# A four-layer attention and mixture-of-experts kernel: layers 2 to 4 of a pair as one instruction stream per batch instead of one for both

## The chip, the cores and the metric

The kernel runs on one core of a Trainium2 chip. A core has four compute engines that run their own instruction streams side by side: PE (TensorE, matrix products and transposes into PSUM banks), DVE (VectorE), ACT (ScalarE, activation functions and copies) and POOL (GpSimd). SP (SyncE) computes nothing here; its stream issues the DMA transfers. The streams meet only through semaphores: an instruction increments one when it is done, another engine waits for a value.

The metric is the device time of one execution, in microseconds (us), as the median of several runs.

## What is computed

Eight batches, each of 128 rows of width 128, go through four layers in fp32. A layer is a cross-attention on a context of 120 rows (x) and a feed-forward part (f). Cut to what matters:

```python
def layernorm(x): return (x - mean(x)) / sqrt(var(x) + 1e-5)

# for each of the 8 batches; ctx is [120, 128]
x = x + attention1(q=ctx @ .., k=ctx @ .., layernorm(x))              # L0X: one head
n = layernorm(x)                                                       # L0F: 8 heads x 8 experts
gate_v, gate_o = top2_sigmoid(n @ sel_v), top2_sigmoid(n @ sel_o)      #   [128, 8 heads, 8 experts]
for h in range(8):
    v   = sum(gate_v[:, h, e] * (n @ v_w[h, e]) for e in range(8))     #   128x128 products
    o   = softmax(q_h @ k_h.T) @ v
    x  += sum((gate_o[:, h, e] * o) @ o_w[h, e] for e in range(8))
x = x + softmax_masked(16 heads of 8)(layernorm(x), ctx)               # L1X
x = x + LN(gelu(layernorm(x) @ ternary(W_fc))) @ ternary(W_proj)       # L1F
x = x + softmax_masked(2 heads of 64, q and k normalized)(..)          # L2X
n = layernorm(x)                                                       # L2F: 8 experts
x = x + sum(top2_softmax(n @ Wg)[:, e] * (gelu(n @ W1[e] + b1) @ W2[e] + b2) for e in range(8))
x = x + softmax(16 heads of 64, plus a bias)(layernorm(x), ctx)        # L3X
n = layernorm(x)                                                       # L3F: grouped top 2 of 8
x = x + routed_experts(n, sigmoid gates, best group of 2) + relu(n @ up)**2 @ down
```

## The kernel before

**Two halves and four pairs.** The eight batches are taken in four pairs; the two batches of a pair are called lanes 0 and 1. Layer 0 (L0X and L0F) is the front half of a pair, and the three other layers (L1X to L3F) are its back half. The two halves have buffers of their own: names with `f_` and `gated`, `weights`, `gates_of` belong to the front half, `bank`, `wide_a`, `wide_b`, `small`, `route` to the back half. So the front half of pair k+1 runs while the back half of pair k runs.

**What the front half is.** It opens with a chain of short dependent steps: layer norm (`f_xn`), attention of one head, layer norm, routing of 64 experts on DVE (`f_group`, `f_route`), softmax exponentials of 8 heads per lane on ACT (line 1039), then the gates are turned by PE (`f_gateT`), written to memory and read back broadcast over partitions (`gated<-gates_of`, 512 KB each). After this chain come the experts, 32 groups of gated products: DVE multiplies `gated` by `f_xnT`, PE runs 8 products of 128x128 for each. They are the bulk of PE's work.

**What the back half is.** `back_pair(pair)` of an engine writes the steps of both lanes in lockstep: each stage stands as `for lane in LANES`. Its softmaxes of 16 heads are 16 exponentials per lane on ACT (line 1103, one per head, with the row sum read out), the transposes and products of PE taken 4 heads at a time. L1F uses GELU (line 1155), L2F uses GELU with a bias in 16 pieces per lane (line 1211); GELU and exponential need different tables in ACT, and the compiler puts an ACT_TABLE_LOAD where they change. The routings of L2F and L3F are computed for both lanes by one set of small DVE instructions on tiles of 128x16 (`route`, `per_group`).

**What sets the order.** Each engine executes one stream. `front_steps()` is a generator that writes the front half of all pairs, with a `yield` after every step. `weave` returns `ahead()`, which stands between the steps of `back_pair`, and takes from the string `AHEAD` for this engine how many front steps are written at this place. So there are two sequences, front and back, and in the back one both lanes move together. The last pair's back half has no front half beside it: this stretch is called the tail.

**Before the first pair** stands a setup: folded weights of layer 0, and as late setup, woven with the front half of pair 0, the ternary weights of L1F (`abs_sum`, `threshold`, `w_L1f`), the mask lengths (`lens`, line 1604), `qkn`, and the products that belong to them (line 459, a helper through which most products go).

**Products that keep PE running.** `keep_warm` (its products go to `f_bank` out of `w_const`, 512 columns, with no reader) stands at five places of the tail, 11 products in all; two more products stand in the front half of pair 0, into `bank`.

**Transfers.** The context of the next pair is loaded for both lanes by one transfer (`ctx_back`, 120 KB), the result of a pair is stored by one (128 KB).

Of the kernel before, what the change touches and what calls it, by code (L numbers as in the profile page):

```python
# [6 lines left out]
ALU = mybir.AluOpType  # L7
# [34 lines left out]
AHEAD = {  # L42
# [28 lines left out]
def build(nc, x_in, ctx_in, q_mask, k_mask, pair_mask, packs, experts, gates_of, out):  # L71
    with ExitStack() as stack:
# [246 lines left out]
        with nc.Block() as block:  # L319
# [41 lines left out]
            def _(pe):  # L361
# [7 lines left out]
                for half in range(2):  # L369
# [5 lines left out]
                    last.then_inc(setup_products, 1)  # L375


        def weave(engine, steps):
            counts = iter(AHEAD.get(engine, "").split())

            def ahead():
# [1623 lines left out]
```

## Time and profile before

| | us |
|---|---|
| median of 3 runs | 759.89 (757.17 to 760.71) |
| the profiled execution | 758.24 |
| its span in the trace | 756.9 |
| busy in the span: PE | 680.3 (90%), 5496 instructions |
| busy: DVE | 495.9 (66%), 1289 instructions |
| busy: ACT | 369.6 (49%), 1281 instructions |
| busy: POOL | 188.8 (25%), 256 instructions |

The span is cut into nine stretches for reading: the start, with the front half of pair 0 alone up to 116 us; then three times a stretch in which the opening chain of the next pair's front half runs beside the first layers of the current pair's back half (116 to 168, 289 to 336, 458 to 507 us), each followed by one in which the front half's experts run beside the rest of the back half (168 to 289, 336 to 458, 507 to 626 us); and the tail (626 to 757 us). "PEclk" is the clock that the chip granted to PE, as a share of 2.4 GHz. A matrix product of fp32 stands in the trace as two PE instructions, a transpose as one.

### The profile page before, as it was taken

Reading aid. Unit: us, or ns where it says so; the run is one execution under the profiler, and the core shown is the slowest. Engines: PE = TensorE matmul, PEld = TensorE weight load, DVE = VectorE, ACT = ScalarE, POOL = GpSimd, SP = SyncE. Lnnn points to the kernel's source line nnn. Section 1 sums busy time; section 2 is a strip of 40 time slices with the busy share of each in tenths; the row PEclk is TensorE's granted clock in tenths of the full one; section 3 lists DMA queues with packets and bytes.
Section 4 is the critical chain, followed back from the end, with each engine's and each line's share of the span. In section 5 each row is a group of like instructions: output and inputs, shape, how many; then the busy total and the mean of one; then the engine's idle time right before and its main releaser. Section 6 shows DMA issues by size and latency. Waiting matters only on the chain.

```text
span 756.9 us, 14486 instructions
## 1 busy us (share of the span) xinstructions
PE 680.3 (90%) x5496; PEld 599.8 (79%) x5496; DVE 495.9 (66%) x1289; ACT 369.6 (49%) x1281; POOL 188.8 (25%) x256
## 2 busy tenths in 40 slices
PE   5759998899999898889999997999999996879887
PEld 4559996769999795759999995769999894557675
DVE  1946557948776848948767667858767477155635
ACT  2420204971363833971366535872365635636473
POOL 1000006342101606342201416423101407420130
PEclk9869998699999999899999998899999998899969
DMA  9659992039836511057833703049816400000000
GB/s 349 288 187 349 374 382 63 2 125 353 303 104 229 168 57 29 1 169 270 308 116 133 266 1 118 3 146 347 292 65 207 156 29 7 1 1 1 2 1 8
DMA packets 33189, 113.71 MB, mean 150 GB/s; under 512 B 3680, under 2 KB 7264, under 8 KB 32736
## 3 DMA queue, kind: packets, MB, share of 16 engines
q1 hardware_dynamic: 33120, 112.78, 42.3%
q8 instruction: 44, 0.72, 0.4%
q14 instruction: 25, 0.20, 0.1%
HBM read 111.72 MB, written 1.05 MB: 149 GB/s over the span
## 4 chain that ended last, share of the span: by engine, by line
PE 59%; DVE 18%; ACT 10%; POOL 5%; DMA 3%; issue 2%; SPq 0%; POOLq 0%; DVEq 0%
PE f_bank L459 29%; PE bank L459 26%; ACT wide_b L1103 4%; DMA gated<-gates_of 3%; DVE gated L1431 3%; PE bank L655 2%; DVE f_route L1431 1%; POOL rstd L1322 1%; DVE max_neg L1690 1%; DVE wide_b L1434 1%; DVE x L1434 1%; ACT f_b L1039 1%; ACT wide_a L988 1%; POOL wide_b L1331 1%; PE f_bank L552 1%
## 5 line engine op out<-in xcount | busy, mean ns | idle before, releaser
L459 PE MATMUL f_bank<-weights,gated 128*128 128x128 f32 x2048 | 245.2, 278 | 9.1 <-DVE gated L1431 8.8
L459 PEld LDWEIGHTS f_bank<-weights,gated 128*128 128x128 f32 x2048 | 237.0, 194 | 13.4 <-issue 11.4
L1103 ACT ACTIVATE wide_b<-wide_b,max_neg 128x120 f32<-128x120 f32 x272 | 103.6, 386 | 25.5 <-DVE max_neg L1690 19.7
L1322 POOL TENSOR_TENSOR rstd<-var_eps,w_const 128x1 f32<-128x1 f32 (+1 forms) x56 | 44.6, 796 | 253.4 <-DVE var_eps L1427 253.2
L1431 DVE TENSOR_TENSOR gated<-gated,f_b 128x1024 f32<-128x1024 f32 x64 | 81.5, 1296 | 29.0 <-ACT f_b L988 15.4
L1331 POOL TENSOR_TENSOR wide_b<-wide_b,row_inv 128x480 f32<-128x480 f32 x64 | 72.0, 1130 | 104.9 <-DVE row_inv L1695 104.7
L1431 DVE TENSOR_TENSOR gated<-gated,f_xnT 128x1024 f32<-128x1024 f32 x64 | 76.8, 1224 | 19.6 <-DMA gated<-gates_of 19.4
L988 ACT ACTIVATE wide_a<-bank 120x512 f32<-120x512 f32 (+4 forms) x109 | 57.3, 550 | 52.4 <-PE bank L655 14.4
L655 PE MATMUL bank<-w_const,wide_b 128*120 128x128 f32 x256 | 46.5, 323 | 13.2 <-POOL wide_b L1331 12.9
L1286 POOL TENSOR_TENSOR f_rstd<-f_var_eps,w_const 128x1 f32<-128x1 f32 x24 | 13.3, 559 | 175.3 <-DVE f_var_eps L1427 175.1
L1103 ACT ACTIVATION_READ_ACCUMULATOR wide_b<-wide_b,max_neg 128x1 f32 x272 | 52.2, 192 | 0.0
L655 PEld LDWEIGHTS bank<-w_const,wide_b 128*120 128x120 f32 x256 | 34.3, 162 | 22.5 <-issue 21.7
L1690 DVE TENSOR_REDUCE max_neg<-wide_b 128x4 f32<-128x480 f32 x64 | 41.8, 653 | 2.2
L988 ACT ACTIVATE xnT<-bank 128x128 f32<-128x128 f32 x48 | 12.1, 277 | 57.9 <-PE bank L644 57.7
L459 PE MATMUL bank<-wide_a,v 120*32 120x128 f32 (+1 forms) x512 | 37.2, 297 | 3.5 <-ACT wide_a L988 3.4
L988 ACT ACTIVATE f_v<-f_bank 128x512 f32<-128x512 f32 x16 | 9.5, 597 | 56.4 <-PE f_bank L459 56.4
L459 PEld LDWEIGHTS bank<-wide_a,v 120*32 120x32 f32 (+1 forms) x512 | 30.0, 134 | 8.9 <-issue 6.9
L1211 ACT ACTIVATE wide_a<-bank,w_L2f 128x128 f32<-128x128 f32 x128 | 34.3, 452 | 0.0
L459 PE MATMUL bank<-xnT,w_L2f 128*128 128x128 f32 x256 | 30.4, 276 | 0.0
L1431 DVE TENSOR_TENSOR x<-bank,x 128x128 f32<-128x128 f32 x24 | 6.9, 288 | 35.7 <-PE bank L459 35.6
L1434 DVE SCALAR_TENSOR_TENSOR wide_b<-bank,w_L3x 128x480 f32<-128x480 f32 x32 | 20.5, 639 | 14.8 <-PE bank L459 14.8
L1434 DVE SCALAR_TENSOR_TENSOR x<-bank,gate,x 128x128 f32<-128x128 f32 x64 | 22.4, 351 | 11.4 <-PE bank L459 9.6
(236 smaller groups left out, 1202.2 us busy)
## 6 DMA issues: line engine op xcount, KB each, us to landing
gated<-gates_of SPq DMA_DIRECT2D x128, 512.0 KB, 6.3
weights<-in_experts SPq DMA_DIRECT2D x64, 512.0 KB, 6.8
w_L2f<-in_L2f SPq DMA_DIRECT2D x1, 2124.0 KB, 15.0
w_L3x<-in_L3x SPq DMA_DIRECT2D x1, 2108.0 KB, 19.1
wide_b<-in_raw0f SPq DMA_DIRECT2D x1, 1024.0 KB, 5.6
w_L3f<-in_L3f SPq DMA_DIRECT2D x1, 1000.0 KB, 21.8
w_L1f<-in_L1f SPq DMA_DIRECT2D x1, 516.0 KB, 9.3
x_next<-in_x SPq DMA_DIRECT2D x4, 128.0 KB, 5.9
```

The lines of the kernel that those rows point to most:

```text
L459: return nc.tensor.matmul(o, lhsT, rhs, start=first, stop=last)
L552: last = nc.tensor.transpose(f_bank[lane][:, 128 * c:128 * c + 128], f_b[lane][:, 128 * h:128 * h + 128], ident)
L655: last = nc.tensor.transpose(bank[lane][(1, 2, 0, 1)[i]][0:K, 128 * c:128 * c + 128], wide_b[lane][:, K * h:K * h + K], ident)
L988: return nc.scalar.activation(o, i, ACT.Identity, bias=bias, scale=scale)
L1103: last = nc.scalar.activation(p, p, ACT.Exp, bias=max_neg[lane][:, h:h + 1], accum_out=row_sum[lane][:, h:h + 1])
L1211: last = nc.scalar.activation(wide_a[lane][:, at:at + 128], bank[lane][(1, 0, 2, 1)[i]][:, 128 * c:128 * c + 128], ACT.Gelu, bias=part["L2 ...
L1286: nc.gpsimd.tensor_tensor(f_rstd[lane][:, :], f_var_eps[lane][:, :], part["const", "minus_half"][:, 0:1], ALU.pow)\
L1322: nc.gpsimd.tensor_tensor(rstd[lane][:, cols], var_eps[lane][:, cols], part["const", "minus_half"][:, 0:cols.stop - cols.start], ALU.pow)\
L1331: nc.gpsimd.tensor_tensor(p3, p3, row_inv[lane][:, 4 * i:4 * i + 4].unsqueeze(2).broadcast_to([128, 4, K]), ALU.mult).then_inc(probs_norme ...
L1431: return nc.vector.tensor_tensor(o, a, c, op)
L1434: return nc.vector.scalar_tensor_tensor(o, a, scalar, c, op0, op1)
L1690: nc.vector.tensor_reduce(max_neg[lane][:, 4 * i:4 * i + 4], s3, AX.X, ALU.max, negate=True)\
```

## The change

1. Each engine's stream is woven out of three generators instead of two: the front half, and the back half of lane 0 and of lane 1. `ORDER` holds a string for each engine with one letter per step: `f`, `0` or `1`. The back half of a lane ends with pair k and goes on with pair k+1 without regard to the other lane.
2. `back_pair(pair)` becomes `back_lane(pair, lane)`. The order inside a lane's sequence is nearly the old one; on ACT the transposed probabilities are taken 2 pieces behind the exponentials of the same lane (before: 4 behind over both lanes), on DVE the inverse sums 1 behind (before: 2).
3. The routings of L2F and L3F are written for each lane on tiles of 128x8. Per pair L2F's goes from 19 to 30 DVE instructions and L3F's from 31 to 56, over four pairs 144 more. The step semaphores `max_taken` and `gate_ready` are kept for each lane.
4. `ctx_back` is loaded, and the output stored, for each lane (60 KB and 64 KB), with a semaphore of its own for each lane's load.
5. The 11 `keep_warm` products of the tail are gone. The two in the front half of pair 0 stay.
6. ACT_TABLE_LOADs in the stream of ACT: 17 before, 35 after. For the back halves of the four pairs 4, 4, 4 and 4 before; 10, 10, 8 and 6 after.
7. `pair_lens`, a small copy on POOL, is made for each lane (4 instructions more).

The diff, cut to its core:

```diff
-AHEAD = {
-    "PE": "10 6 5 15 28 0 8 0 0 5 0 2 0 1 2 2 1 0 2 0 1 2 0 0 0 0 0 7 0 0 1 0 2 1 2 1 3 1 0 0 0 1 1 0 0 0 1 0 0 "
...
+ORDER = {
+    "PE": "ffffff00fff0f0ffffffffffffffffffffffffffffffffffffffffffffffffffffff001010ff00ff1ff0ff100f00ff1ff01f"
...
-        ctx_back_loaded = sem("ctx_back_loaded")
+        ctx_back_loaded = [sem(f"ctx_back_loaded{lane}") for lane in LANES]
...
-        def weave(engine, steps):
-            counts = iter(AHEAD.get(engine, "").split())
-
-            def ahead():
-                for _ in range(int(next(counts, 0))):
-                    next(steps, None)
-
-            def rest():
+        def weave(engine, front, lane0, lane1):
+            streams = {"f": front, "0": lane0, "1": lane1}
+            for stream in ORDER.get(engine, ""):
+                next(streams[stream])
+            for steps in streams.values():
                 for _ in steps:
                     pass
-            return ahead, rest
...
+                    if pair + 1 < PAIRS:
-                        for lane in LANES:
-                            sp.wait_ge(kv_psum[lane], kv_psum.upto(L2X, 3, pair))
-                        cols = slice(2 * K * (pair + 1), 2 * K * (pair + 2))
-                        sp.dma_start(ctx_back[:, :], ctx_in[:, cols]).then_inc(ctx_back_loaded, 16)
-                        ahead()
+                        sp.wait_ge(kv_psum[lane], kv_psum.upto(L2X, 3, pair))
+                        cols = slice(K * (2 * pair + 2 + lane), K * (2 * pair + 3 + lane))
+                        sp.dma_start(columns(ctx_back, lane, K), ctx_in[:, cols]).then_inc(ctx_back_loaded[lane], 16)
+                        yield
...
-                    link(tt(as_lanes[3], as_lanes[3], of_lanes(part["const", "first"]), ALU.mult))
+                    link(tt(r[3], r[3], first, ALU.mult))
+                    yield
                     link(nc.vector.tensor_reduce(worth[1], halves[3], AX.X, ALU.max))
...
+                weave("DVE", front_steps(), back_steps(0), back_steps(1))
```

What the strings move is shown at three places. A name's last digit is the lane or, for `bank`, lane and bank; line numbers of the two kernels differ.

**DVE at the start**, where the late setup meets the front half of pair 0. Before, from the second lane's variance to the routing of layer 0:

```order
L1427 TENSOR_SCALAR f_var_eps_1<-f_mean_var_1 128x1
L1428 TENSOR_SCALAR f_xn_0<-f_x_0,f_mean_var_0,f_rstd_0 128x128
L1428 TENSOR_SCALAR f_xn_1<-f_x_1,f_mean_var_1,f_rstd_1 128x128
L1428 TENSOR_SCALAR threshold<-bank00 128x2
L1427 TENSOR_SCALAR threshold<-threshold 128x2 x2
L1427 TENSOR_SCALAR wide_a_1<-w_L1f,threshold 128x512
L1427 TENSOR_SCALAR w_L1f<-w_L1f,threshold 128x512
L1431 TENSOR_TENSOR w_L1f<-w_L1f,wide_a_1 128x512
```

Now, from the first row of the late setup to the first lane's `f_x`, which stands ahead of all the rows above except the setup's own:

```order
L1332 TENSOR_SCALAR threshold<-bank00 128x2
L1331 TENSOR_SCALAR threshold<-threshold 128x2 x2
L1331 TENSOR_SCALAR wide_a_1<-w_L1f,threshold 128x512
L1331 TENSOR_SCALAR w_L1f<-w_L1f,threshold 128x512
L1335 TENSOR_TENSOR w_L1f<-w_L1f,wide_a_1 128x512
L1331 TENSOR_SCALAR wide_a_1<-w_L1f,threshold 128x512
L1331 TENSOR_SCALAR w_L1f<-w_L1f,threshold 128x512
L1335 TENSOR_TENSOR w_L1f<-w_L1f,wide_a_1 128x512
L1372 RECIPROCAL f_row_inv_1<-f_row_sum_1 128x1
L1507 TENSOR_REDUCE lens<-wide_b_1 128x8 x2
L1338 SCALAR_TENSOR_TENSOR qkn<-w_L2x 128x1
L1338 SCALAR_TENSOR_TENSOR f_x_0<-f_bank0,f_row_inv_0,f_x_bias_0 128x128
```

The ternary weights have moved from behind the front half's second layer norm to ahead of it, and `lens` and `qkn`, which before stood behind the first `gated` tile, stand there too.

**ACT beside the opening chain of pair 1's front half** (`f_b` are its exponentials, `f_gateT` the gates' turn; the rest belongs to the back half of pair 0). Before:

```order
L1031 ACTIVATE f_group<-f_group 128x64
L1039 ACTIVATE f_b_0,f_row_sum_0<-f_bank0,f_max_neg_0 128x128 x4
L1039 ACTIVATE f_b_1,f_row_sum_1<-f_bank1,f_max_neg_1 128x128 x4
L1103 ACTIVATE wide_b_1,row_sum_1<-wide_b_1,max_neg_1 128x120 x4
L988 ACTIVATE wide_a_1<-bank12 120x512
L988 ACTIVATE wide_a_0<-bank00 120x512
L1039 ACTIVATE f_b_0,f_row_sum_0<-f_bank0,f_max_neg_0 128x128 x4
L1039 ACTIVATE f_b_1,f_row_sum_1<-f_bank1,f_max_neg_1 128x128 x4
L988 ACTIVATE f_gateT0<-f_bank0 128x128
```

Now:

```order
L975 ACTIVATE f_group<-f_group 128x64
L983 ACTIVATE f_b_0,f_row_sum_0<-f_bank0,f_max_neg_0 128x128 x4
L983 ACTIVATE f_b_1,f_row_sum_1<-f_bank1,f_max_neg_1 128x128 x4
L1089 ACT_TABLE_LOAD
L1089 ACTIVATE wide_b_0<-bank01 128x512
L932 ACTIVATE wide_a_0<-bank02 120x384
L932 ACTIVATE wide_a_1<-bank10 120x512
L983 ACT_TABLE_LOAD
L983 ACTIVATE f_b_0,f_row_sum_0<-f_bank0,f_max_neg_0 128x128 x4
L932 ACTIVATE wide_a_1<-bank11 120x512
L983 ACTIVATE f_b_1,f_row_sum_1<-f_bank1,f_max_neg_1 128x128 x4
L932 ACTIVATE f_gateT0<-f_bank0 128x128
```

Lane 0 is already in L1F when the second half of the front half's exponentials comes, so GELU stands between two groups of exponentials, with a table load on either side.

**PE in the tail, at L2F of the last pair** (`xnT` by `w_L2f` are the experts' first products). Before:

```order
L459 MATMUL bank01<-xnT_0,w_L2f 128x128 x4
L459 MATMUL bank11<-xnT_1,w_L2f 128x128 x4
L459 MATMUL bank00<-xnT_0,w_L2f 128x128 x4
L459 MATMUL bank10<-xnT_1,w_L2f 128x128 x4
L459 MATMUL bank02<-xnT_0,w_L2f 128x128 x4
L459 MATMUL bank12<-xnT_1,w_L2f 128x128 x4
```

Now:

```order
L460 MATMUL bank01<-xnT_0,w_L2f 128x128 x4
L460 MATMUL bank00<-xnT_0,w_L2f 128x128 x4
L777 MATMUL bank12<-w_const,wide_b_1 120x128 x2
L460 MATMUL bank02<-xnT_0,w_L2f 128x128 x4
L460 MATMUL bank11<-wide_a_1 128x128 x2
L460 MATMUL bank01<-xnT_0,w_L2f 128x128 x4
L460 MATMUL bank00<-w_L2f,wide_a_0 128x128 x8
L644 MATMUL bank10<-w_const,xn_1 128x128
```

Lane 0's experts stand beside the end of lane 1's L2X (turned probabilities, output product, layer norm), where before both lanes' experts stood side by side.

## Rows read from the trace of the kernel before

**Rows 1.** Busy time by stretch: start:end and length, each engine, PE clock, DMA.

```profile
core 0: us, PE busy (x) PEld busy (x) DVE busy (x) ACT busy (x) POOL busy (x), PEclk, DMA share, GB/s
0.00:60.00 60.00, 37.75 (x209) 32.60 (x210) 32.33 (x77) 18.32 (x66) 3.26 (x10) 0.83 0.72 270
60.00:116.00 56.00, 55.67 (x495) 55.35 (x494) 32.40 (x31) 5.08 (x10) 0.00 (x0) 1.00 0.99 374
116.00:168.00 52.00, 45.47 (x279) 34.18 (x278) 35.95 (x97) 38.50 (x151) 25.86 (x42) 0.84 0.14 39
168.00:289.00 121.00, 117.59 (x1081) 112.41 (x1082) 88.61 (x222) 52.49 (x168) 22.50 (x23) 1.00 0.57 197
289.00:336.00 47.00, 38.60 (x259) 28.59 (x260) 33.86 (x94) 35.40 (x146) 24.54 (x40) 0.93 0.16 41
336.00:458.00 122.00, 119.80 (x1097) 114.02 (x1095) 86.39 (x224) 55.34 (x172) 25.94 (x23) 1.00 0.53 185
458.00:507.00 49.00, 43.27 (x274) 31.24 (x275) 35.06 (x99) 38.27 (x151) 25.28 (x41) 0.86 0.24 70
507.00:626.00 119.00, 117.13 (x1085) 112.36 (x1083) 85.37 (x221) 52.28 (x167) 23.26 (x23) 1.00 0.53 188
626.00:757.00 131.00, 105.05 (x727) 79.10 (x726) 65.96 (x233) 73.93 (x253) 38.13 (x57) 0.86 0.01 3
```

**Rows 2.** DVE at the start in order of time: start, duration, instruction, idle before.

```profile
15.11 0.34 DVE L1428 TENSOR_SCALAR f_xn<-x_next,f_mean_var,f_rstd 128x128 f32<-128x128 f32 x1
...
21.07 0.35 DVE L1434 SCALAR_TENSOR_TENSOR f_x<-f_bank,f_row_inv,f_x_bias 128x128 f32<-128x128 f32 x1
...
24.12 0.15 DVE L1428 TENSOR_SCALAR threshold<-bank 128x2 f32<-128x2 f32 x1
...
28.14 0.41 DVE L1490 TENSOR_REDUCE f_group<-f_route 128x32 f32<-128x256 f32 x1
...
49.79 1.23 DVE L1431 TENSOR_TENSOR gated<-gated,f_xnT 128x1024 f32<-128x1024 f32 x1 [8.14 <-DMA gated<-gates_of]
50.94 2.21 DVE L1604 TENSOR_REDUCE lens<-wide_b 128x8 f32<-128x960 int32 x2
```

**Rows 3.** DVE, first and last instruction of pair 1's opening front chain.

```profile
120.21 0.34 DVE L1428 TENSOR_SCALAR f_xn<-x_next,f_mean_var,f_rstd 128x128 f32<-128x128 f32 x1
...
167.10 1.22 DVE L1431 TENSOR_TENSOR gated<-gated,f_xnT 128x1024 f32<-128x1024 f32 x1
```

**Rows 4.** The tail's chain of waits: shares by line, then pieces (start, length).

```profile
by line: PE bank L459 41.5%; ACT wide_b L1103 15.2%; issue 3.6%; PE bank L655 3.4%; POOL rstd L1322 2.4%; PE f_bank L459 2.0%; ACT wide_a L988 1.9%; DVE wide_b L1431 1.8%; DVE small L1917 1.6%; POOL wide_a L1339 1.5%; DVE stats L1626 1.2%; 
...
634.42 7.67 ACT wide_b L1103 x40
...
660.83 1.28 ACT L1155
662.13 0.61 ACT wide_b L1155
...
689.55 14.80 PE bank L459 x130
...
715.44 7.68 ACT wide_b L1103 x40
```

**Rows 5.** Busy time in short stretches, columns as in rows 1.

```profile
52.00:56.00 4.00, 4.00 (x21) 4.00 (x21) 4.00 (x6) 0.00 (x0) 0.00 (x0) 0.50 0.99 392
...
640.00:660.00 20.00, 16.87 (x107) 10.95 (x106) 6.60 (x21) 13.67 (x50) 10.59 (x18) 0.73 0.00 1
...
689.00:705.00 16.00, 15.51 (x136) 15.11 (x136) 7.91 (x33) 10.86 (x38) 0.00 (x0) 1.00 0.00 1
```

**Rows 6.** Groups of instructions: two of the tail, one of the whole span.

```profile
L459 PE MATMUL f_bank<-w_const 128*128 128x512 f32 x22 | 11.9, 663 | 0.0
...
L988 ACT ACTIVATE wide_a<-bank 120x512 f32<-120x512 f32 x16 | 9.0, 588 | 4.3 <-PE bank L655 4.2
...
L1431 DVE TENSOR_TENSOR route<-route,per_group 128x16 f32<-128x16 f32 x44 | 7.7, 175 | 1.5
```

More of the change, by code:

```diff
@@ new lines, in back_lane @@
+                    yield
+                    turn_x(lane, L3X, xn[lane])
+                    yield
+                    for half in range(2):
+                        pe.wait_ge(xnT_ready[lane], xnT_ready.upto(L3X, 1, pair))
+                        for c in range(4):
+                            at = 512 * half + 128 * c
+                            last = mm(bank[lane][1 + half][:, 128 * c:128 * c + 128],
+                                      part["L3x", "wq"][:, at:at + 128], xnT[lane][:, :])
+                        last.then_inc(q_psum[lane], 1)
+                        yield
@@ new lines, in back_lane @@
+                    last.then_inc(hidden_psum[lane], 1)
+                    yield
+                    pe.wait_ge(hidden_ready[lane], hidden_ready.upto(L3F, 3, pair))
+                    for c in range(4):
+                        mm(bank[lane][1][:, 0:D], wide_a[lane][:, 128 * c:128 * c + 128],
+                           part["L3f", "down"][:, 128 * c:128 * c + 128], c == 0, False)
+                    yield
+                    pe.wait_ge(hidden_ready[lane], hidden_ready.upto(L3F, 5, pair))
@@ L1169, in back_pair @@
-                    ahead()
+                        for n in range(4 + behind):
+                            if n < 4:
+                                exponentials(lane, layer, n, range(4 * n, 4 * n + 4))
+                                yield
+                            if n >= behind:
+                                take_transposed(layer, n - behind, lane)
+                                yield
+                    act.wait_ge(kv_psum[lane], kv_psum.upto(L1X, 1, pair))
+                    copy(small[lane][:, 128:128 + K], bank[lane][1][:, 0:K], bias=part["L1x", "bk"])\
+                        .then_inc(kv_ready[lane], 1)
@@ L1172, in take_keys_l3 @@
+                    act.wait_ge(turned_psum[lane], turned_psum.upto(L2X, 1, pair))
+                    copy(wide_a[lane][:, 1408:1408 + K], bank[lane][2][:, 0:K], scale=qkn[:, :])\
+                        .then_inc(turned_ready[lane], 1)
+                    yield
                     def take_keys_l3(half, lane):
@@ L1188, in back_pair @@
-                    ahead()
-                    for lane in LANES:
-                        exponentials(lane, L2X, 0, range(H2X))
-                    ahead()
-                    for lane in LANES:
-                        act.wait_ge(pT_psum[lane], pT_psum.upto(L2X, 1, pair))
-                        copy(wide_a[lane][0:K, 256:512], bank[lane][2][0:K, 0:256]).then_inc(pT_ready[lane], 1)
-                    ahead()
-                    for lane in LANES:
-                        take_xT(lane, L2F)
@@ new lines, in back_lane, with back_steps @@
+                    yield
+                    inverse_root(lane, L2X, 2, one)
+                    yield
+                    inverse_root(lane, L2X, 3, slice(0, 2))
+                    yield
+                    inverse_root(lane, L2F, 1, one)
+                    yield
+                    inverse_root(lane, L3X, 1, one)
+                    yield
+                    yield from normalise_probs(L3X)
+                    inverse_root(lane, L3F, 1, one)
+                    yield
+                def back_steps(lane):
+                    for pair in range(PAIRS):
+                        yield from back_lane(pair, lane)
@@ new lines, in back_lane @@
+                    for h in range(H2X):
+                        p = wide_b[lane][:, K * h:K * h + K]
+                        last = ts(p, p, row_ok[lane][:, 2 + h:3 + h], row_inv[lane][:, h:h + 1], ALU.mult, ALU.mult)
+                    last.then_inc(normed[lane], 1)
+                    yield
+                    add_output(lane, L2X, bank[lane][1][:, 0:D])
+                    yield
+                    norm_apply(lane, L2F)
+                    yield
+                    dve.wait_ge(gate_psum[lane], gate_psum.upto(L2F, 1, pair))
@@ L1872, in back_pair @@
-                    r = [route[:, i, 0:both] for i in range(7)]
-                    halves = [r[i].rearrange("p (g e) -> p g e", e=4) for i in range(7)]
-                    worth = [per_group[:, i, 0:4] for i in range(4)]
+                        yield from mix_half(half, lane)
+                        yield
+                    dve.wait_ge(out_psum[lane], out_psum.upto(L2F, 3, pair))
+                    x_done(lane, L2F, tt(x[lane][:, :], bank[lane][1][:, 0:D], x[lane][:, :], ALU.add))
+                    yield
```

1245 lines of the change are left out of this document (541 added, 704 removed), and 20 rows, old and new, of the table AHEAD.

## The prediction, made before the changed kernel ran

> **What bounds the kernel now.** I read the busy time by stretch first [rows 1], since the totals of a kernel with four repeated pairs mix places with different limits. There are three kinds. In the expert stretches (168 to 289, 336 to 458, 507 to 626, and 60 to 116) PE is busy 97 to 99% of the time at a clock of 1.00; DVE follows with at most 73%, ACT with 45%. PE is the bound there, and a change moves them only by the PE work that stands in them. In the three chain stretches (116 to 168, 289 to 336, 458 to 507) no engine is full: in the first PE has 45.47 of 52 us, at a clock of 0.84, ACT 38.50, DVE 35.95. What ends last is the opening chain of the next pair's front half, since no expert product can run before the first gated tile: in pair 1 from 120.21 to 167.10, 46.9 us [rows 3]. In pair 0, where nothing of a back half is beside it, the same chain runs from 15.11 to 49.79 [rows 2]: 34.7 us. So up to 12 us of each chain stretch is what the back half's steps put between the chain's, in the orders of ACT, DVE and PE. The third kind is the tail, 131 us with the last pair's back half alone: PE 105.05 busy, with 11.9 of it products that nobody reads [rows 6], ACT 73.93, DVE 65.96, clock 0.86. The chain of waits there [rows 4] goes to and fro: PE products 41.5%, exponentials 15.2%. Its long pieces are 40 ACT rows in 7.67 us (20 exponentials and their sums), 130 products in 14.80, 40 ACT rows in 7.68. Each of them carries both lanes' work, after which the other engines get going again: the lockstep is what makes the tail long.
>
> **The start, +5 us (0 to +7).** DVE makes the ternary weights in 4.0 us, from 24.12 to 28.14 [rows 2], in a place where the front half's routing was on its way through PE and ACT anyway; the f_group that follows is then ready without a wait. Now this work, `lens` (2.21) and `qkn` (0.15) stand ahead of `f_x_0`, which ran at 21.07. They begin when `abs_sum` has gone through PE. In the new order `abs_sum` can start after the first lane's maximum, and its product is not behind 512-column products any more, so the block can start near 20.9: 20.9 + 4.0 + 2.4 gives `f_x_0` near 27.3, 6.2 late. Behind it the chain is as before, but only 0.7 of setup work stands between it and f_group instead of 4.0, less about 2 us that the routing needs on PE and ACT after `f_xn`: late by 6.2 - 3.3 + 2 = 5 at f_group. The 2.4 us of `lens` that leave their old place behind the first gated tile [rows 2] return nothing, since PE there runs at a clock of 0.50 and is full [rows 5]. The lower end is that f_group waited for something else than DVE; the upper end is the full 6.2 and a little.
>
> **Expert stretches, -6.3 us.** I counted the PE work of both orders between a pair's first and last expert product, at 0.111 us an instruction (119.80 over 1097 gives 0.109, 14.80 over 130 gives 0.114, [rows 1, 4]). Before: 108.9, 111.2 and 108.9, together 329.0, for 358 us of trace, a factor of 1.09. After: 97.0, 108.1 and 118.1, together 323.2. The difference, 5.8, times 1.09 is 6.3. It is no work saved: back-half products have moved from these stretches into the chain stretches.
>
> **Chain stretches, -2 us (-12 to +10).** They get that work: 31.5, 30.0 and 32.2 before, 35.0, 33.0 and 31.9 after, where they have room (45.47 busy of 52, part of it at half clock). What decides is what stands on ACT between the chain's steps. Of the back half's exponentials, 0.384 us each with their sums (7.67 over 20, [rows 4]), there were 32 in each of the three; now 32, 16 and 16. Other copies of the back half, 0.59 at most [rows 6], were 7, 11 and 10, and are 20, 19 and 15. Pair 1: 13 copies at about 0.35 and two table loads of 1.28 [rows 4] are 7.1, of which some 2 are hidden by DVE and POOL steps of the chain: +5. Pair 2: -6.1 and +3: -3. Pair 3: -6.1 and +2: -4. The lower end is that all three come down to 43 us each, the upper that copies and table loads cost in full.
>
> **Table loads and routing in the expert stretches, +3 us (0 to +20).** Of the 18 new loads 2 are in the chain stretches, 2 in the tail; 14 are here, 18 us of ACT. The 144 new DVE instructions at 0.175 [rows 6] are 25 us, 19 of them here. ACT has 52.49 of 121 and DVE 88.61 of 121 busy [rows 1], so both fit under PE: the cover is that PE always has expert products or the other lane's to run. They cost only where PE's order has the next back-half product too early; +3 for that. Without this cover it would be 18 us.
> The Trainium skill ("ScalarE: Activation LUTs", "What ACT_TABLE_LOAD costs") puts a switch at 2.66 us, load and drain. By it 18 loads would be 48 us instead of 23. The trace doesn't agree for this kernel: the load at 660.83 took 1.28 and the GELU behind it began at 662.13 [rows 4]. The same page's "Table sets: the hidden batching unit" wants calls batched by set, and speaks against this change.
>
> **The tail, -15 us (-24 to -7).** `keep_warm` is 2.0% of the chain [rows 4], 2.6 us; two more table loads are 2.6: they cancel. What is left is the stagger: lane 0 is about half a layer ahead, so that lane 1's exponentials run while PE has lane 0's products. On the chain, the three long pieces lose their second half, (7.67 + 14.80 + 7.68) / 2 = 15.1. Shorter pieces lose theirs too, but the engines collide: ACT's 73.93 + 2.6 can't be undercut, and each lane's own chain is longer than that. I take the 15.1, a tail of 116. The lower bound is a tail of 107, the upper that half of the 15 is lost. The transfers per lane and the copies on POOL cost nothing: DMA is at 0.01 in the tail, 0.14 to 0.24 in the chain stretches [rows 1], where the context is needed. The last store is of 64 KB instead of 128.
>
> **The sum.** +5 - 6.3 - 2 + 3 - 15 = -15.3 on the profiled 758.24, so 742.9, a ratio of 0.980; on the median of 759.89 that is 744.5. I say **744**.
>
> **The rivals.**
> A, the forecast: 732 to 753. 0.42.
> B, the chain stretches come down to what the front half needs: with fewer exponentials before its gates, all three are 43 us instead of 46.9 and the like (-12 instead of -2), and the tail gives 20 and more. 744 - 10 - 6 = 728, 712 to 732. For it: pair 0's chain took 34.7. Against it: more PE and copy work now stands in these stretches. 0.24.
> C, the clock eats the tail's gain. After the 8.1 us in which DVE waited for the gates of pair 0, and PE for DVE [rows 2], PE ran at 0.50, at least from 52 to 56 [rows 5]; in the tail it was at 0.73 between 640 and 660 but at 1.00 in L2F's 16 us [rows 5], behind keep_warm products. Without these L2F and L3X could begin at 1.2 GHz: 14.8 us of products would take some 5 more, and as much again over the other places. 744 + 10 = 754, and up to 764 if in the middle the loads show too. 0.16.
> The Trainium skill ("TensorE: Matmul & The Clock Gate", "HAM oscillation") describes such falls of the clock in kernels whose PE idles between tiles. By it the removal of `keep_warm` costs; the removed products themselves are the 11.9 us of PE.
> D, slower: the fixed orders bind. One stream's step that isn't ready holds the two others on its engine. The price is the cover above: with two table loads and the routing of each lane held ahead of front steps in each pair, ACT and DVE steps that gate expert products come late, 18 us of loads that are no longer hidden, and the start's 5, with half the tail's gain left: 744 + 18 + 7.5 = 770. It decides as soon as PE's busy share in the expert stretches falls under 92%. Against it: 97% now, and DVE gets there only to about 78%. 0.18.
>
> **How the numbers follow.** Range for 8 in 10: from 718, inside B, to 764, the end of C; that leaves out D and the end of B. A alone is 732 to 753. A change of 0.5%, 3.8 us, is about what a measurement can tell from none. Faster by more than that (under 756.1): A, B and half of C, 0.71 with a little of D's near side. Same: the rest of C, and where D is mild, 0.12. Slower 0.17.
>
> **What would show it.** In the trace after: f_group of pair 0 near 33 instead of 28.14; first gated tile of pair 0 near 55. The expert stretches PE-busy over 96% at 1.00, about 2 us shorter each on average, the first shortest. Pair 1's opening chain longer than 46.9, those of pairs 2 and 3 shorter. Tail from the last expert product to the end 110 to 120 us, with L2F of lane 0 beside L2X of lane 1. Wrong would be: a tail over 125 (C, if its clock is under 0.8; else the chain of one lane is longer than I think), or PE idle in the expert stretches (D).

## The result, and the profile after

The changed kernel is slower by 1%: 767.0 us (764.7 to 771.6, 4 runs) against 759.8 for the kernel before (4 runs), a ratio of 1.010 with a 95% interval of 1.007 to 1.013. The forecast was 744, in a range of 718 to 764; the time lies outside, and on the other side of 759.8. The profiled execution took 764.72, with a span of 763.4.

The trace of the changed kernel, busy time by stretch, columns as in [rows 1]. The cuts are at its own first and last expert products, so the stretches are the same nine: start, experts of pair 0, then chain and experts three times, then the tail.

```profile
0.00:56.50 56.50, 31.69 (x163) 25.91 (x163) 26.65 (x72) 18.75 (x68) 3.26 (x10) 0.88 0.63 235
56.50:121.80 65.30, 63.54 (x546) 62.85 (x547) 38.63 (x35) 4.78 (x8) 0.55 (x1) 0.98 0.97 365
121.80:177.70 55.90, 45.70 (x307) 34.44 (x305) 39.46 (x117) 43.48 (x158) 27.03 (x46) 0.91 0.13 36
177.70:286.70 109.00, 104.70 (x943) 100.26 (x942) 79.92 (x199) 48.09 (x145) 17.13 (x17) 1.00 0.61 220
286.70:336.50 49.80, 41.55 (x319) 32.12 (x317) 38.25 (x123) 38.09 (x142) 20.63 (x35) 0.96 0.19 55
336.50:461.00 124.50, 117.89 (x1039) 110.58 (x1040) 89.39 (x231) 60.90 (x183) 27.83 (x29) 0.99 0.55 187
461.00:505.40 44.40, 38.51 (x311) 30.56 (x310) 36.49 (x123) 34.98 (x130) 19.13 (x31) 1.00 0.18 49
505.40:640.40 135.00, 130.40 (x1158) 119.94 (x1156) 99.50 (x268) 69.09 (x214) 32.43 (x37) 1.00 0.48 163
640.40:763.40 123.00, 95.44 (x702) 73.52 (x702) 73.11 (x268) 75.66 (x253) 37.43 (x57) 0.86 0.01 3
```

The kernel before has the same cuts at 51.2, 116.8, 168.5, 288.4, 336.6, 457.3, 507.7 and 625.9, close to those of [rows 1]. That gives the difference by stretch, and beside it what the prediction had:

| | before | after | difference | forecast |
|---|---|---|---|---|
| start and experts of pair 0 | 116.8 | 121.8 | +5.0 | +5 |
| chain stretches | 51.7, 48.2, 50.4 | 55.9, 49.8, 44.4 | -0.2 | -2 |
| expert stretches | 119.9, 120.7, 118.2 | 109.0, 124.5, 135.0 | +9.7 | -3.3 |
| tail | 131.0 | 123.0 | -8.0 | -15 |
| span | 756.9 | 763.4 | +6.5 | -15.3 |

Two rows of four are far off, and in both a gain is missing. In the expert stretches PE has fewer instructions (3140 against 3263 in [rows 1]) at the same clock, but hardly less busy time (353.0 us against 354.5), and it stands idle for 15.5 of 368.5 us, where in [rows 1] it is 7.5 of 362: PE's busy share fell from 97 or 98% to 95 to 97%. In the tail PE is only 95.44 busy, ten less than before, at the same clock of 0.86; the `keep_warm` products that are gone were 11.9 of it [rows 6]. (They stood at six places of the tail, two at each of five and one at the sixth, not at five places as the part on the kernel before has it.)

The start, in DVE's order of time (start, duration, instruction): what [rows 2] has at 21.07, 28.14 and 49.79.

```profile
27.24 0.34 DVE L1338 SCALAR_TENSOR_TENSOR f_x<-f_bank,f_row_inv,f_x_bias 128x128 f32<-128x128 f32 x1
...
32.84 0.42 DVE L1394 TENSOR_REDUCE f_group<-f_route 128x32 f32<-128x256 f32 x1 [0.33 <-ACT f_route L932]
...
55.11 1.23 DVE L1335 TENSOR_TENSOR gated<-gated,f_xnT 128x1024 f32<-128x1024 f32 x1 [8.76 <-DMA gated<-gates_of]
```

The three groups of table loads of largest cost in the view of groups, 29 of the 34 behind the first, and then the chain of waits of the second expert stretch where they stand thickest (start, length, what; a row "ACT L1135" without a name is a table load).

```profile
L1046 ACT ACT_TABLE_LOAD x12 | 15.4, 1283 | 0.2
...
L1135 ACT ACT_TABLE_LOAD x10 | 12.8, 1283 | 0.2
...
L1089 ACT ACT_TABLE_LOAD x7 | 9.0, 1283 | 0.1
```

```profile
415.90 3.13 ACT wide_b L1046 x16
419.03 0.19 ACT route L1128
419.22 0.02 issue
419.24 1.28 ACT L1135
420.52 0.01 issue
420.54 1.14 ACT wide_a L1135 x4
421.67 0.02 issue
421.69 1.28 ACT L1046
...
422.99 1.62 ACT wide_b L1046 x8
...
427.10 1.28 ACT L1135
...
428.39 3.20 ACT wide_a L1135 x12
```

One lane is in the softmax of L3X, the other in the GELUs of L2F, and ACT begins three table loads within 8 us, with the chain of waits on it without a break from 415.90 to 431.6. Over the whole span the chain holds 21 loads, 27 us; that of before holds 4, 5.1 us (the expectation of the second run below says 3).

### The profile page after: what moved, and what is told of

It is laid out like the page before. It is cut to its first block, busy times and chain, and to the rows that moved or that the text cites. A ratio compares the mean times of both kernels' runs of the same rounds, so it can differ in the third digit from the quotient of the medians.

```text
span 763.4 us, 14661 instructions
## 1 busy us (share of the span) xinstructions
PE 669.4 (88%) x5474; PEld 590.2 (77%) x5474; DVE 521.4 (68%) x1433; ACT 393.8 (52%) x1299; POOL 185.4 (24%) x260
## 4 chain that ended last, share of the span: by engine, by line
PE 54%; ACT 17%; DVE 15%; POOL 4%; DMA 4%; issue 3%; SPq 0%; DVEq 0%; POOLq 0%
PE f_bank L460 27%; PE bank L460 22%; ACT wide_b L1046 5%; DMA gated<-gates_of 4%; ACT wide_a L1135 2%; PE bank L655 2%; DVE f_route L1335 2%; DVE gated L1335 2%; ACT f_b L983 2%; PE f_bank L553 1%; ACT wide_a L932 1%; ACT L1135 1%; POOL wide_b L1247 1%; DVE wide_b L1338 1%; DVE max_neg L1579 1%
## 5 line engine op out<-in xcount | busy, mean ns | idle before, releaser
L460 PEld LDWEIGHTS f_bank<-weights,gated 128*128 128x128 f32 x2048 | 238.0, 194 | 19.1 <-issue 15.2
L1239 POOL TENSOR_TENSOR rstd<-var_eps,w_const 128x1 f32<-128x1 f32 (+1 forms) x56 | 34.8, 622 | 282.3 <-DVE var_eps L1331 282.1
L1335 DVE TENSOR_TENSOR gated<-gated,f_b 128x1024 f32<-128x1024 f32 x64 | 78.4, 1233 | 31.4 <-DMA gated<-gates_of 24.9
L1335 DVE TENSOR_TENSOR gated<-gated,f_xnT 128x1024 f32<-128x1024 f32 x64 | 79.1, 1249 | 28.3 <-DMA gated<-gates_of 27.8
L655 PE MATMUL bank<-w_const,wide_b 128*120 128x128 f32 x256 | 41.5, 294 | 8.8 <-POOL wide_b L1247 8.6
L655 PEld LDWEIGHTS bank<-w_const,wide_b 128*120 128x120 f32 x256 | 30.4, 147 | 18.3 <-issue 14.1
L460 PE MATMUL bank<-xnT,w_L2f 128*128 128x128 f32 x256 | 34.8, 289 | 2.4 <-ACT wide_a L1135 2.4
L932 ACT ACTIVATE wide_b<-bank 128x480 f32<-128x480 f32 (+2 forms) x40 | 21.0, 524 | 30.5 <-PE bank L460 30.5
L1135 ACT ACTIVATE wide_a<-bank,w_L2f 128x128 f32<-128x128 f32 x128 | 34.6, 403 | 0.1
L460 PEld LDWEIGHTS bank<-xnT,w_L2f 128*128 128x128 f32 x256 | 31.8, 201 | 3.5 <-ACT wide_a L1135 3.4
L460 PE MATMUL bank<-w_L2f,wide_a 128*128 128x128 f32 x256 | 31.6, 278 | 0.4 <-ACT wide_a L1135 0.4
```

The source lines that it names most:

```text
L460: return nc.tensor.matmul(o, lhsT, rhs, start=first, stop=last)
L655: last = nc.tensor.transpose(bank[lane][(1, 2, 0, 1)[i]][0:K, 128 * c:128 * c + 128], wide_b[lane][:, K * h:K * h + K], ident)
L932: return nc.scalar.activation(o, i, ACT.Identity, bias=bias, scale=scale)
L1135: last = nc.scalar.activation(wide_a[lane][:, at:at + 128], bank[lane][(1, 0, 2, 1)[i]][:, 128 * c:128 * c + 128], ACT.Gelu, bias=part["L2 ...
L1239: nc.gpsimd.tensor_tensor(rstd[lane][:, cols], var_eps[lane][:, cols], part["const", "minus_half"][:, 0:cols.stop - cols.start], ALU.pow)\
L1335: return nc.vector.tensor_tensor(o, a, c, op)
```

## The experiments

All are on one core, each against the kernel before on the same chip (759.4 to 760.0). The theory at this point, T: the loads of activation tables, which the sum had at 3 us in the expert stretches and 5 elsewhere, are on the path. Its rival, W: the loads lie beside other work, and it is the weave of three fixed streams that makes PE wait.

**Both kernels without table loads.** The same edit in each:

```diff
-                    nc.scalar.activation(wide_b[lane][:, 0:512], bank[lane][1][:, :], ACT.Gelu)\
+                    nc.scalar.activation(wide_b[lane][:, 0:512], bank[lane][1][:, :], ACT.Relu)\
...
-                                                        bank[lane][(1, 0, 2, 1)[i]][:, 128 * c:128 * c + 128], ACT.Gelu,
+                                                        bank[lane][(1, 0, 2, 1)[i]][:, 128 * c:128 * c + 128], ACT.Relu,
```

> The changed kernel with both GELUs replaced by ReLU, which lives in the same table as the exponential: the stream of ACT then has 1 table load instead of 35, all else stands where it stood (the values of L1F and L2F are not the reference's). Theory T (table loads): the chain of waits of the changed kernel holds 21 loads of 1.28 us, 27 us; without them the kernel takes 741 to 747, some 20 to 26 less than 767. Rival W (weave): the loads lie beside other work, and it is the order of three streams that makes PE wait; then at most 5 us go and it stays at 762 or more.

> The kernel before with both GELUs replaced by ReLU (values of L1F and L2F are not the reference's), 1 table load instead of 17. Its chain of waits shows 3 loads, 3.8 us. Theory T: 754 to 757, 3 to 6 less than 760, so that without loads the changed kernel is the faster by 10 or more. Rival W: the same 754 to 757 here, and the changed kernel stays slower than this one.

Measured: the changed kernel 748.0, 0.984 of before (0.981 to 0.988), 19.1 less than with its loads. The kernel before 756.7, 0.996 (0.994 to 0.999), 3.2 less. (ReLU gives other values than GELU; ACT's rows of the two differ by 6 ns at most, 403 against 397 for the 128x128 pieces, so that apart from the loads the streams cost the same.) Expert stretches and tail of the changed kernel without loads, and then the expert stretches of the kernel before without them:

```profile
174.60:280.90 106.30, 104.11 (x943) 100.10 (x942) 79.58 (x199) 39.15 (x138) 17.17 (x17) 1.00 0.64 224
...
329.30:449.10 119.80, 118.37 (x1039) 111.91 (x1040) 89.66 (x231) 50.46 (x175) 27.82 (x29) 0.98 0.58 193
...
493.50:624.10 130.60, 129.24 (x1158) 119.65 (x1157) 98.62 (x269) 60.14 (x207) 32.24 (x37) 1.00 0.50 169
624.10:744.20 120.10, 92.59 (x702) 71.73 (x702) 72.90 (x268) 68.09 (x247) 37.50 (x57) 0.89 0.01 3
```

```profile
167.20:287.30 120.10, 117.39 (x1079) 112.13 (x1079) 87.55 (x219) 48.35 (x163) 22.89 (x23) 1.00 0.58 200
...
336.20:456.10 119.90, 119.05 (x1096) 113.79 (x1094) 85.32 (x222) 50.10 (x166) 25.90 (x23) 1.00 0.54 186
...
506.00:623.00 117.00, 116.02 (x1081) 112.01 (x1080) 84.71 (x220) 48.05 (x163) 22.45 (x23) 1.00 0.54 189
```

The loads cost the changed kernel 11.8 in the expert stretches (368.5 against 356.7), where PE is back at 98 to 99% busy, 4.8 in the chain stretches and 2.9 in the tail. T holds, with its numbers a little too good (748.0 is just above its 747, and it wanted 10 or more between the two kernels), and W falls: without loads the changed kernel is the faster one by 8.7 (748.0 against 756.7). 34 loads cost 19.1, 0.56 each; in the kernel before 16 cost 3.2, 0.20 each. The difference is 15.9 for 18 more loads, 0.88 for each that the change adds.

**The changed code in the old order.** The strings put every step where the kernel before had it. The edit is the strings alone; the first row of DVE's:

```diff
-    "DVE": "fff0ff0f0fff0f0fffffffffffffffffffffffffffffffffffffffffffffffff0ff01000f000ff0ff11fff11f01101fff1ff"
+    "DVE": "ffff0ffffff0fffffffffffffff0fffff0fffffffffffffffffffffffff0ffffffff01fffff0ff10f01f100f11ff00f1f1ff"
```

> The changed kernel's code (routing, loads and stores for each lane, no keep_warm) with strings that put every step where the kernel before had it, both lanes in lockstep: 17 table loads. Theory T: what the code for each lane costs alone is small, 760 to 767 (routing of each lane on DVE up to 5, keep_warm 0 to 3). Rival R (routing): the 144 more DVE instructions are on the path in lockstep and cost most of their 25 us, 775 or more; then the changed kernel's 767 would hide a gain of the order.

> As the lockstep kernel, but the steps of the last pair's back half in the changed kernel's order of the lanes. The changed kernel's tail was 8 us shorter than before's, with 2 table loads more in it. Both theories: 6 to 9 less than the lockstep kernel, its tail from the last expert product to the end near 123 instead of 131.

Measured: lockstep 774.3, 1.020 of before (1.016 to 1.023); with the last pair staggered 761.1, 1.002 (1.000 to 1.004). In lockstep the tail took

```profile
632.70:771.60 138.90, 103.19 (x707) 81.75 (x705) 74.58 (x275) 74.46 (x253) 38.42 (x58) 0.79 0.01 3
```

and staggering the last pair is worth 13.2 in the medians, 11.5 in the tail (127.4), in this code, which has no `keep_warm`. That is larger than what either theory expected of it, and close to the 15.1 of the prediction. But the code itself, in the old order, costs 14.5: twice the 0 to 7 that T expected of it, and just short of the 15 and more of rival R. Two pieces of it were then measured.

**keep_warm.** Taken out of the kernel before, and put back into the changed one:

```diff
-                    if pair == PAIRS - 1:
-                        keep_warm(2, f_bank[0])
```

```diff
+                    if pair == PAIRS - 1 and lane == 1:
+                        keep_warm(2, f_bank[0])
                     turn_x(lane, L1F, xn[lane])
```

> The kernel before without its 11 keep_warm products in the tail. They are 2.6 us of its chain, and the lockstep kernel, which lacks them and has the routing for each lane, had a tail of 138.8 instead of 131.1. If the clock is what they are for, 3 to 6 more than 760 with a clock under 0.86 in the tail, and the lockstep kernel's 7.7 are mostly this; if not, 0 to 3 less, and the 7.7 are the routing.

> The changed kernel with the 11 keep_warm products back, at lane 1's six places of the last pair. Theory K (the clock eats the tail's gain): the tail falls from 123 by 4 or more and its clock rises from 0.86. Rival: the products stand in the way of the other lane; 0 to 3 us longer.

Measured: before without the products 763.8, 1.005 (1.004 to 1.007); the changed kernel with them 777.4, 1.022 (1.017 to 1.028), 10.4 more than without. The tails, of before without them and of after with them:

```profile
627.00:763.80 136.80, 101.57 (x707) 81.16 (x704) 66.00 (x233) 74.11 (x253) 38.26 (x57) 0.81 0.01 3
```

```profile
649.40:780.40 131.00, 104.31 (x724) 77.51 (x724) 72.89 (x268) 76.06 (x253) 37.50 (x57) 0.89 0.01 3
```

In the kernel before the products pay: 3.8 in the medians, 5.8 in the tail, whose clock falls from 0.86 to 0.81 without them. Between 680 and 700 us, where L2F begins, it was 0.91 with them and is 0.66 without (681 to 701). So in lockstep their removal wasn't free, and in the profiled executions it is 5.8 of the 7.9 by which the lockstep kernel's tail is longer. In the staggered tail the same products raise the clock too, from 0.86 to 0.89, and make it 8.0 longer: PE's busy time goes up by 8.9 (104.31 against 95.44), and they are 6.8% of the tail's chain of waits, 8.9 us, where in the kernel before they are 2.0% [rows 4]. Theory K had the sign of the clock right and that of the time wrong, and its rival's 0 to 3 was too little. A second reading of the same two rows: with the products in both, the staggered tail is as long as the lockstep one, 131.0. What staggering gains and what the products cost can't be priced one without the other. (In that profiled execution the clock was lower in the start as well, 0.74, ahead of any change; the 10.4 of the medians is therefore less sure than its interval says.)

The Trainium skill ("TensorE: Matmul & The Clock Gate", "HAM oscillation") describes how PE's clock falls when PE waits between pieces of work. The rows agree with it in direction, by 0.05 and 0.03 of the tail's mean clock; whether the products pay depends on what stands behind them.

**The routing for each lane.** In the changed kernel, 152 of the DVE instructions left out (1281 in the trace against 1433; the expectation says 136):

```diff
-                    link(nc.vector.tensor_reduce(worth[0], halves[0], AX.X, ALU.max))
-                    link(tt(halves[3], halves[0], to_halves(worth[0]), ALU.is_equal))
...
                         for nth in range(2):
+                            if nth == 1:
+                                yield
+                                yield
+                                return
```

> The changed kernel without the group selection of L3F and without the second of the top 2 in both routings: 136 DVE instructions less, about as many as the kernel before has; values of L2F and L3F are not the reference's, all steps stand where they stood. Theory R (the routing for each lane is on the path where PE is idle, in the tail and the chain stretches): 4 to 8 less than 767, half of it in the tail. Rival: hidden beside the other lane, under 2 us.

Measured: 765.5, 1.008 (1.005 to 1.010), 1.5 less, which is within the scatter of the changed kernel's own runs (764.7 to 771.6). With lanes staggered the routing is hidden or nearly so, as the rival said and as the prediction's cover had it. In lockstep it isn't: of the staggered-tail kernel's last chain stretch, and of the hybrid's below, in which the first three pairs' routing is computed for both lanes at once:

```profile
461.60:516.50 54.90, 46.33 (x279) 34.68 (x279) 39.13 (x107) 38.90 (x153) 26.37 (x42) 0.81 0.12 40
```

```profile
459.40:509.90 50.50, 42.86 (x279) 30.76 (x277) 36.09 (x99) 38.88 (x153) 26.32 (x42) 0.90 0.16 44
```

**The late setup of pair 0** back in its old place:

```diff
-    "Activation": "fffff00fff0f0ffffffffffffffffffffffffffff0011000ff00ff0ff01010f01ff01f1ff01fffff001f1ff1ff0ff0f10101"
+    "Activation": "fffffffffffffffffff00ffffffffffff00ffffff0011000ff00ff0ff01010f01ff01f1ff01fffff001f1ff1ff0ff0f10101"
```

> The changed kernel with the late setup of pair 0 back where the kernel before has it, on PE (the first 71 letters of its string), ACT (39) and DVE (64); the rest of the strings as changed. Step S of the prediction (the start costs 5): the first expert product at 51 instead of 56.5, and the 5 us reach the end, 762. Rival: something behind it, a transfer or the expert stretch of pair 0, takes the time back, and it stays at 766.

Measured: 762.4, 1.003 (1.001 to 1.005), 4.6 less. Nothing behind it takes the time back, and the first expert product starts at 52.5, 4.0 earlier.

**Is it the number of loads, or where they stand?** Two kernels have the changed code in strings found by a search that moved steps and summed durations taken from the traces; a third is the kernel before with 18 loads more in the expert stretches:

```diff
                                 .then_inc(f_v_ready[lane], 1)
+                            if pair > 0:
+                                at = 8 * (pair - 1) + 4 * half + 2 * lane
+                                nc.scalar.activation(idle_act[:, at:at + 1], part["const", "ones"][:, 0:1], ACT.Gelu)
+                                nc.scalar.activation(idle_act[:, at + 1:at + 2], part["const", "ones"][:, 0:1], ACT.Exp)
                             yield
```

> The changed kernel's code with other strings: steps of all five engines moved by a search that started at the changed kernel's strings and priced every instruction by its duration in the traces, a table load at 1.28 us. 32 table loads after the first instead of 34, so nearly all remain. Theory T2 (what costs is where the loads stand, not how many there are): 745 to 755, most of the 19 us that the run without loads gave back, with few loads on the chain of waits. Rival N (each load costs wherever it stands): 762 or more.

> The same search, started at the lockstep strings with the last pair staggered (761.1): lanes mostly together in the first three pairs, 20 loads after the first. If few loads beat hidden ones this is the faster of the two; by the search's own sum both are within 2 us of each other, 745 to 757.

> The kernel before with 18 table loads more, 35 as the changed kernel has: in pairs 1 to 3, behind each of the 4 copies of the front half's values on ACT, a GELU and an exponential of one column into a tile that nobody reads. All stand in expert stretches; with their activations they are some 27 us of ACT. Theory P (place): under PE's expert products, with both lanes in lockstep, they are hidden as the prediction had it: 760 to 765. Rival N (each load costs wherever it stands, 0.6 to 1 us as the changed kernel's 19 us for 34 suggest): 771 or more, and then the prediction's cover was wrong for the kernel before as well.

Measured: the searched orders 793.8, 1.046 (1.041 to 1.051), and 796.5, 1.048 (1.043 to 1.053), both far over all that was expected. They tell nothing about loads. What they do show is that a sum of mean durations is no guide to a fixed order here: it had put both within 2 us of each other, between 745 and 757. In the first, PE's clock in the chain stretches was 0.90 to 0.93 (0.91 to 1.00 in the changed kernel) and 0.81 in a tail of 137.9 (0.86 in 123.0). Of the 27 us between the two profiled executions 15 are in the tail and 10 in the chain stretches. How much of that is the clock was not tried.

The kernel before with 18 loads more: 773.3, 1.019 (1.017 to 1.020). Its expert stretches:

```profile
169.10:295.40 126.30, 119.80 (x1080) 114.74 (x1080) 87.50 (x219) 60.42 (x179) 23.00 (x23) 0.97 0.55 189
...
343.70:467.80 124.10, 120.23 (x1096) 114.21 (x1094) 85.43 (x222) 63.15 (x185) 25.88 (x23) 1.00 0.53 180
...
518.50:640.60 122.10, 118.15 (x1080) 113.75 (x1080) 84.68 (x219) 60.82 (x180) 22.34 (x23) 0.99 0.53 181
```

All 13.8 us of it are there: 126.3, 124.1 and 122.1 against 119.9, 120.7 and 118.2. ACT has 60 of 126 us busy, and some 27 us of work put on an engine that is half idle cost 13.8. P falls: expert products on PE don't hide table loads in the old order either. Of N only the size is borne out, 0.77 for each load, and that with the 24 one-column activations of 0.2 us that stand between them. That a load costs so much wherever it stands is not shown: the kernel's own 16 cost 0.20 each, and the added ones stand bunched behind the front half's copies, up to two loads and two activations in a row, 3 us, and two such blocks with a single copy of 0.6 us between them in each pair. The three stretches lost 6.4 (at a clock of 0.97), 3.4 and 3.9. Loads spread one by one in the same stretches were not tried.

**A version that beats both.** The staggered-tail kernel, with the routings of pairs 0 to 2 computed at once for both lanes, in lane 1's steps:

```diff
+                    joint = pair < PAIRS - 1
...
                     def top2():
+                        if joint:
+                            if lane == 0:
+                                for _ in range(4):
+                                    yield
+                                return
+                            left = rj[0]
...
+                    if joint and lane == 0:
+                        for _ in range(10):
+                            yield
+                    elif joint:
+                        yield from joint_l3()
```

> As e4 (lockstep strings, last pair staggered, one sequence per lane), but the routings of L2F and L3F of pairs 0 to 2 are computed for both lanes at once again, as in the kernel before; only the last pair's are per lane. In e4 the last chain stretch was 54.9 against 50.4 before, with both lanes' L3F routing on its chain of waits. If that is the routing, the stretch is back near 50.5 and the kernel takes 755 to 758, faster than both; rival: it is the loads and stores per lane or the order, and it stays at 761.

Measured: 753.7 (749.5 to 755.0), 0.994 of before (0.992 to 0.995), a little below what was expected, and 7.4 less than the staggered-tail kernel. The last chain stretch is back at 50.5 (row above), the second at 47.9 against 50.2, with loads and stores still for each lane; PE's waits for the mixed output of L3F's experts (`small`), which follows the routing on DVE, are 0.7 us in the last one instead of 3.8. The tail, of the staggered-tail kernel and of the hybrid, whose code there is the same:

```profile
634.80:762.20 127.40, 97.89 (x707) 75.83 (x705) 75.13 (x275) 76.18 (x255) 38.17 (x58) 0.84 0.01 3
```

```profile
627.50:749.40 121.90, 92.79 (x706) 71.98 (x704) 73.38 (x269) 75.77 (x255) 38.05 (x58) 0.91 0.01 3
```

They differ by 5.5, at a clock of 0.84 against 0.91. The hybrid's seven runs, one program, were granted between 0.934 and 0.961 over their whole span, and the highest clock went with the shortest time (0.961, 749.5). So a single profiled execution can be off by that much in the tail, and of the tails above only differences that the medians carry too should be believed.

## Why the prediction was wrong, point by point

**What bounds the kernel** was read right as far as it went: PE in the expert stretches, a chain in the three others, the lockstep in the tail. What was missing is that a bound engine at 97% doesn't hide another engine's work by that alone. My reading, which no run separates: in a fixed order it is full because everything else arrives just in time.

In the table above the forecast and the span differ by 21.8 us. Some 7 of it are the table loads in the expert stretches, 6 the PE work there, 7 the tail and 2 the chain stretches: three terms failed by about the same amount, the first by its mechanism, the two others by their size.

**The start** was right in its size and its way: f_x at 27.24 (forecast 27.3), f_group at 32.84 (33), the first gated tile at 55.11 (55), and 4.6 us when undone.

**Table loads and routing in the expert stretches** is the step that failed by its mechanism. "Both fit under PE: the cover is that PE always has expert products or the other lane's to run" gave +3 for 14 loads and the routing. The routing half of it holds (1.5 for 152 instructions, in all stretches). The loads cost 11.8 there and those of before 1.8 (358.8 against 357.0 with the ReLU), so the new ones cost 10.0. That is inside the term's own range of 0 to 20, whose upper end is "without this cover"; the value of 3 had no row behind it. The experiment that would have told is the one that put 18 loads into the kernel before: 13.8 us.

**The expert stretches** had a second error of nearly the same size. Without loads in either kernel they took 356.7 in the changed one and 357.0 in the kernel before: of the 6.3 forecast, 0.3. The counted work was right in its shape: with the loads out of both kernels the first stretch shrank by 13.8, and the third grew by 13.6. But the factor of 1.09 between counted and traced time was not constant: 1.12 to 1.15 with loads, 1.10 to 1.11 without. The price of an instruction wasn't either: between the same cuts PE was busy for 352.8 us with 3256 instructions before and for 353.0 with 3140 after, 0.108 and 0.112 each. Why is open.

**The chain stretches** came out at -0.2 against -2. Pair by pair: +4.2 (forecast +5), +1.6 (-3), -6.0 (-4). Of these, loads are 3.4, 1.4 and 0. So the first was right, with more of it from the loads and less from the copies than the sum had; the second was 4.6 worse than forecast, of which the loads explain 1.4, and the fewer exponentials bought nothing that the rows show.

**The tail** gave 8.0 of the 15. Its mechanism is shown in the code without `keep_warm`, where staggering the last pair gives 11.5 to 13.2. The term that failed is the one that was said to cancel: `keep_warm`, priced at its 2.0% of the chain, 2.6 us of gain. A share of the chain is what a piece takes, not what the others would take without it. In lockstep taking the products out costs 3.8 to 5.8; in the staggered order it saves 8.0 to 10.4. So the steps from the one tail to the other, in profiled executions, are +5.8 (products out), +2.1 (code for each lane), -11.5 (last pair staggered) and -4.4 (from there to the changed kernel, with the last pair in the same order and the clock 0.86 instead of 0.84). In another order of the steps each would have another size, and the last is no more than the 5.5 by which two executions of one tail code differ.

**The chances.** A, B and half of C add up to 0.74, not 0.71, so those of "same" and "slower" were a little too high for the rest.

**Rival D** was the right case, at 0.18: orders that bind, loads no longer hidden, the start's 5, half the tail's gain, 770. Its sign to look for was wrong: it was to decide when PE's share fell under 92%, and 95 to 97% was enough, since each per cent of 360 us is 3.6 us. Rival C had a part in it. L2F of lane 0 in the last pair does begin at half clock, 0.50 from 693.5 to 697.8, and its first 18 PE instructions take 4.21 us where 0.114 each would make 2.1. But that is 2 us and not ten: over the whole tail the clock was 0.86, as before. Rival B's shorter chain stretches appeared in the third alone (44.4).

**The drain of a table switch**: in the changed kernel each of the 34 loads began 0.01 or 0.02 us after the activation ahead of it, and 24 of them were followed by the next activation after 0.01 or 0.02 (the chain above shows three). So a switch took 1.28 and not the 2.66 us of the Trainium skill ("ScalarE: Activation LUTs", "What ACT_TABLE_LOAD costs"), as the prediction had it from one row. The advice of the same page of the Trainium skill in "Table sets: the hidden batching unit", to batch by set, was right all the same: in the changed kernel 0.56 us of its time for each 1.28 us load, and 0.88 for each that the change added.

One path through the medians, each as its difference from the kernel before: `keep_warm` out +3.8, the rest of the code for each lane in the old order +10.7, the last pair staggered -13.2, all pairs staggered +6.0; together +7.2. The last step holds the start's 4.6 and 16 more loads. Since all loads together cost the changed kernel 19.1, drifting lanes must have given something back in the first three pairs too; the routing, 7.4 in lockstep and 1.5 when staggered, is a likely part of it, but no run separates it.

## What to carry to other kernels

When two streams that were in lockstep are let drift apart, count what the lockstep shared: here the activation tables, the routing and the warming products. Without table loads in either kernel the change would have gained 8.7 us; with them it lost 7.2. Keeping lockstep where another engine is full, and drifting only where nothing else runs, beat both kernels, once the routing was shared again. And don't take a busy share of 97% as a cover for another engine's work: adding a dummy of the suspected cost to the kernel before settles it.

## What was not expected of the hardware

An engine that is busy for 60.42 of 126.3 us cost the kernel half of what was added to it (some 27 us added, 13.8 lost). A table load costs ACT 1.28 us whatever stands around it, with gaps of 0.02 and 0.01 and no further pause. Products that nobody reads, on an engine that is not full, saved 3.8 us in one order of the tail and cost 10.4 in another, with a higher clock in both. The clock of one and the same tail code was 0.84 in one profiled execution and 0.91 in another, with 5.5 us between them.
